# A graph network's edge layer without row gathers: all 50 node blocks in sorted buckets, part of the sort on GpSimd

## The reference

```python
x = layernorm(x + L0(x, src, dst))                    # mean of the sources, then a linear map
x = layernorm(x + L1(x, edge_weight, src, dst))       # two weighted propagations, L1A and L1B
x = layernorm(x + L2(x, edge_weight1, src, dst, ...)) # the edge layer
x = layernorm(x + L3(x, edge_index, ...))             # two SAGE layers, L3A and L3B

def L2(h, e, src, dst, W1, b1, W2, b2):
    m = relu(concatenate([h[src], h[dst], e]) @ W1 + b1) @ W2 + b2
    return segment_sum(m, dst)
```

## Time and profile before

| | us |
|---|---|
| three runs: lowest, median, highest | 3682.96, 3688.67, 3693.33 |
| profiled execution: span from the first to the last instruction | 4015.9 |
| its stages (us from the start): build and L0 | 260 to 1262 |
| L1A and L1B, first to last dense block, with the sort beside | 1262 to 2152 |
| edge layer, with what leads to and from it | 2152 to 3552 |
| L3A and L3B | 3552 to 4016 |
| busy of the span: PE, DVE, POOL, ACT | 3290.8, 2244.4, 1153.0, 1011.7 |

### The profile page before, as it was taken

One profiled execution on the slowest core, in us unless ns is written; L12 is line 12 of the kernel. 1 busy time (PEld: TensorE's weight loads), 2 busy tenths in 40 slices (PEclk: granted clock), 3 DMA queues, 4 the chain that ended last, 5 costly groups with the idle time before them and its releaser, 6 DMA issues.

```text
span 4015.9 us, 126981 instructions
## 1 busy us (share of the span) xinstructions
PE 3290.8 (82%) x56384; PEld 3021.5 (75%) x56384; DVE 2244.4 (56%) x3103; ACT 1011.7 (25%) x2184; POOL 1153.0 (29%) x1012
## 2 busy tenths in 40 slices
PE   0768999999997888888886577777787777789998
PEld 0757999999996888888885466665566565689898
DVE  8974777666767767677776234444454444331122
ACT  0025777777771000000000111111111111110000
POOL 5587000000001000001001665565566555501100
PEclk9987999999997999999997677777778777799999
DMA  4315777777776999988885343343344433369798
GB/s 122 98 38 179 280 282 278 269 275 269 282 284 242 381 394 381 382 362 345 344 357 192 83 108 107 102 113 104 100 117 109 114 100 104 99 275 343 297 372 326
DMA packets 285688, 904.33 MB, mean 225 GB/s; under 512 B 97944, under 2 KB 162702, under 8 KB 256850
## 3 DMA queue, kind: packets, MB, share of 16 engines
q1 hardware_dynamic: 235802, 857.37, 55.4%
q0 software_dynamic: 35520, 36.44, 6.7%
q10 hardware_dynamic: 13832, 2.70, 0.4%
HBM read 644.17 MB, written 252.83 MB: 223 GB/s over the span
## 4 chain that ended last, share of the span: by engine, by line
PE 39%; issue 35%; DVE 9%; DMA 6%; POOL 4%; another core or an unknown queue 2%; POOLq 2%; DVEq 2%; SPq 1%; ACT 0%; ACTq 0%
PE ps L1601 10%; PE ps L1418 7%; PE ps L1413 5%; DMA stream<-a_weights 5%; PE ps L1632 4%; PE ps L1596 4%; PE ps L1635 4%; PE ps L1521 2%; POOL wend L909 2%; POOL stream L916 2%; DVE operand_room L2274 1%; DVE junk L1739 1%; DVE operand_room L2291 1%; DVEq L2299 1%
## 5 line engine op out<-in xcount | busy, mean ns | idle before, releaser
L936 POOL DMA_INDIRECT stream<-table,stream x660 | 794.4, 1204 | 544.9 <-PE ps L1601 322.6
L1370 PE MATMUL ps<-operand_room 64*128 64x50 bf16 (+1 forms) x18750 | 645.6, 222 | 50.4 <-issue 18.1
L1370 PEld LDWEIGHTS ps<-operand_room 64*128 64x128 bf16 x18750 | 618.9, 163 | 81.8 <-issue 29.6
L1418 PE MATMUL ps<-stream,node_room 125*64 125x125 f32 x10000 | 579.2, 277 | 60.2 <-DMA stream<-a_weights 51.1
L1418 PEld LDWEIGHTS ps<-stream,node_room 125*64 125x64 f32 x10000 | 557.2, 140 | 70.9 <-DMA stream<-a_weights 57.5
L1074 ACT CAST stream<-ps 128x500 bf16<-128x500 f32 (+2 forms) x700 | 431.0, 632 | 246.1 <-PE ps L1370 193.2
L1074 ACT COPY stream<-ps 128x500 f32<-128x500 f32 (+2 forms) x700 | 421.5, 618 | 0.0
L1215 ACT ACTIVATE node_room<-ps 128x320 f32<-128x320 f32 x300 | 131.3, 438 | 885.7 <-remote 460.3
L1413 PE MATMUL ps<-operand_room,stream 125*125 125x192 bf16 x3750 | 319.2, 247 | 4.4 <-POOLq L578 4.4
L1413 PEld LDWEIGHTS ps<-operand_room,stream 125*125 125x125 bf16 x3750 | 313.5, 137 | 4.7 <-POOLq L578 4.7
L2356 DVE TENSOR_TENSOR node_room<-slot_f,stream 128x625 f32<-128x625 f32 x240 | 184.1, 809 | 210.9 <-remote 177.6
(11 more groups left out here) (292 smaller groups left out, 4518.3 us busy)
## 6 DMA issues: line engine op xcount, KB each, us to landing
stream<-a_weights SPq DMA_DIRECT2D x100, 3125.0 KB, 15.0
a_weights<-stream SPq DMA_DIRECT2D x500, 312.5 KB
stream<-a_counts SPq DMA_DIRECT2D x100, 1562.5 KB, 9.1
a_counts<-stream SPq DMA_DIRECT2D x500, 156.2 KB
stream<-sorted_edges SPq DMA_DIRECT2D x80, 781.2 KB
node_room<-sorted_edges SPq DMA_DIRECT2D x40, 781.2 KB
stream<-dst_run SPq DMA_DIRECT2D x20, 1031.2 KB
stream<-table,stream POOLq DMA_INDIRECT x660
```

The source lines that it names most:

```text
L936: pool.indirect_dma_start(emsg[s][:, t, :], None, tables[L2][:, :], bass.IndirectOffsetOnAxis(src_t[j % 3][:, at:at + 1], 0))\
L1370: ins = pe.matmul(out if step == 0 else out[:, 1:2], low[s][rows_a, :, t], planes[s][rows_a, t // TI, what, :, t % TI], start=step == 0, s ...
L1418: ins = pe.matmul(ps_sum[SUM_BANK[MATRIX[k]][b]][half:half + D, 0:Q], tab_in_of(k)[0:Q, h, :], a[0:Q, h, :], start=h < 2, stop=h >= NPP - 2)
```

## The change

All 50 blocks are done from sorted buckets. The gathers, the spread of the destination's half and the second relu go, with the run's loads and the stores of the node table and of the split edge values that served them. A *chunk* is now half a block: 5 units of 5 buckets, 100 chunks and 500 units in all; the one-hot rows of a chunk come in one broadcast of 12.8 KB rows to 125 partitions (cut at partition 112), compared against one key. The slot one-hots (of which destination a sorted edge has) are made by VectorE in bf16 for a whole chunk and cast to f32 by GpSimd (units 0, 2, 4 of a chunk) and ScalarE (1, 3), 625 elements each. The sums are in one bank a block, taken block by block.

The sort now does 50 blocks beside 100 dense blocks: `sort_with(n)` puts a half after each. The value splits (`sort_values`) and the product and the folds of the ranks (`fold`, the former L2278 to L2283) are GpSimd's; VectorE keeps the one-hots, the counts, the scan and the products with the values, and waits on `rank_rdy` before it makes the one-hot of the ranks. `hot_src`, `hot_pair` and `run_rank` are double, `run_val` and the keys three deep.

```diff
+        def fold(eng, b):
+            places, pair = hot_src[b % 2], hot_pair[b % 2]
+            ranks = places[:, :, 2:TPAD].rearrange("p s (u t) -> p s u t", t=2)
+            eng.tensor_tensor(ranks, ranks, pair.rearrange("p u s t -> p s u t"), ALU.mult)
+            eng.drain()
+            for to, n, of in ((0, 25, 25), (0, 12, 12), (0, 6, 6), (0, 3, 3), (0, 1, 1), (2, 1, 24)):
+                eng.tensor_tensor(places[:, to:to + n], places[:, to:to + n], places[:, of:of + n], ALU.add)
+                eng.drain()
+            eng.tensor_tensor(run_rank[b % 2].unsqueeze(1), places[:, 0:1, 2:TPAD], places[:, 2:3, 2:TPAD], ALU.add)
+            eng.drain()
...
-            def gather_runs():
...
+            def fold_ranks(b):
+                pool.wait_ge(ranks_counted, b + 1)
+                fold(pool, b)
+                pool.sem_inc(rank_rdy, 1)
+            def beside_weights():
+                for n in range(2 * NPP):
+                    if n % 2 == 0 and n // 2 + 2 < NPE:
+                        sort_values(n // 2 + 2)
+                    if n == 0:
+                        fold_ranks(0)
+                    if n % 2 and n // 2 + 1 < NPE:
+                        fold_ranks(n // 2 + 1)
+                    g = (n - NPP) // GT
+                    if n % GT == GT - 1 and n >= NPP + GT:
                         split_dst(g - 1)
+                split_dst(GROUPS - 1)
...
+            def sort_after(n):                       # TensorE, after dense block n
+                s = n // 2
+                if n % 2:
+                    sort_half(s, 0)
+                    if s:
+                        pe.wait_ge(base_used, min(s + 2, NPE))
+                        sort_slots(s - 1)
+                else:
+                    if n:
+                        sort_half(s - 1, 1)
+                    if s + 1 < NPE:
+                        sort_base(s + 1)
...
+                for w in range(UNITS + 1):           # TensorE, the edge layer
+                    if w < UNITS:
+                        unit(w)
+                    if w:
+                        collect_unit(w - 1)
...
+            def sort_vals(b, h):                     # VectorE
                 if h == 0:
+                    v.wait_ge(rank_rdy, b + 1)
...
+            def sort_with(n):                        # VectorE
+                s = n // 2
+                if n % 2:
+                    sort_vals(s, 0)
+                    if s + 1 < NPE:
+                        sort_counts(s + 1)
+                else:
+                    if n:
+                        sort_vals(s - 1, 1)
+                    else:
+                        sort_counts(0)
+                    if s + 1 < NPE:
+                        sort_pairs(s + 1)
```

More of the change, by code:

```diff
@@ L241, in build_program @@
[L241 to L247, removed]
@@ L255, in build_program @@
[L255 to L257 removed]
+        at = 2 * AROW // 2
+        hots = [in_room(stream, room(HW // 2), HW, BF16) for _ in range(HRING - 1)]
+        hots.append(in_room(node_room, 2 * NPP * D, HW, BF16))
+        slot_key = [in_room(node_room, PWORDS + GT * D + i * NPP, 2 * NPP, BF16).rearrange("p (s t) -> p s t", t=2)
+                    for i in range(3)]
@@ L595, in pieces_out, with turn_of, acc_copies, loads_of @@
             return moves
-        def turn_of(k, mode):
-            return ps_t
+        def turn_of(k, mode, j):
+            if k == L1B and mode == "linear" and j == GT - 1:
+                return bank(3)[:, GT * D:GT * D + P]
+            return ps_t[:, j * P:(j + 1) * P]
+        def acc_copies(b):
+            return sum(a % GT != GT - 1 for a in range(b + 1))
+        def loads_of(c):
+            return 16 * sum(3 + (a % 2 == 0) for a in range(c % HRING, c + 1, HRING))
         def both(eng, run):
@@ L1600, in add @@
-                def add(sums, m, half, rows_of, hots, first, last):
-                    return pe.matmul(sums[half * D:(half + 1) * D, m * Q:(m + 1) * Q], rows_of, hots,
-                                     start=first, stop=last)
-                def collect(c):
-                    i = c // CPB
-                    pe.wait_ge(slot_rdy, c + 1)
-                    pe.wait_ge(relu_done, c + 1)
-                    if c % CPG == 0 and c:
-                        pe.wait_ge(turned_sb, count(WITH_CAT, L2, c // CPG - 1))
-                    for t in range(CHUNK):
-                        at = c % CPB * CHUNK + t
-                        ins = add(ps_acc[0], i % POG, at % 2, emsg[c % MSGS][:, t, :], hot_slot[c % SLOTS][:, t, :],
-                                  at < 2, at >= TILES - 2)
-                    ins.then_inc(s_done, 1)
@@ new lines, in weights_pass @@
+            def weights_pass(k):
+                first = (L1A, L1B).index(k) * NPP
+                for g in range(GROUPS):
+                    for b in range(GT):
+                        if b == 1 and g:
+                            take_sums(k, g - 1, "linear")
+                            finish(k, g - 1, "linear")
+                        sort_with(first + g * GT + b)
+                        if b == GT - 1 and g and k == L1B:
+                            dst_half(g - 1, "linear")
+                        if k == L1A and g == 0 and b == GT - 1:
+                            edge_weights()
+                take_sums(k, GROUPS - 1, "linear")
+                finish(k, GROUPS - 1, "linear")
+                if k == L1B:
+                    sort_with(2 * NPP)
```

880 lines of the change are left out of this document (344 added, 536 removed).

## The result

The changed kernel takes 4001.97 us (median of 4 runs, 3995.78 to 4003.64) against 3687.76 for the kernel before in the same set: 1.0853 times as long, interval 1.0835 to 1.0872. The prediction was 3809, range 3570 to 3910: right in sign, two fifths of the size (+121 for +314), and the time lies above the range. The changed kernel's own profiled execution has a span of 3998.9 us, in line with its runs.

What follows compares the result with a forecast made beforehand. Weights stage taken as near the limits of TensorE and the `a_weights` stream, edge layer as TensorE and GpSimd's gathers holding each other up. 4016 - 470 (edge layer) + 270 (weights stage) + 5 (rest) - 12 (span over runs) = 3809 us; range 3570 to 3910.

Steps and rivals of the forecast that it cites:

- Span and runs: Kernel before: span 327.2 us above the runs, put down to 314.9 us of TensorE gaps in the profiled execution only.
- Rival B: Edge layer: TensorE's gaps are real in every run, so -470 counts against 3689, giving 3494 us; chance 0.08.
- The edge layer, 906: Edge layer: 500 units of 1.78 us at full clock plus 14 us, TensorE setting the pace; 906 for 1376, -470 us.
- The outer bound of +300 for half clock: Edge layer: a third of the units at half clock would cost some 300 us.
- Rival C: Weights stage: TensorE waits for the rank one-hot each pair of blocks, drops to 1.2 GHz; +150, 3959 us; chance 0.12.
- TensorE's added sorts, +55 to +109: Weights stage: 20 more sorts take TensorE 109 us; alone they make the stage some 55 to 109 us longer.
- "half" of cover: Weights stage: at best half of the added sorts' 109 us fits into TensorE's 108 us of idle time.
- rival A: Weights stage: folds hidden in VectorE's gaps, TensorE with the stream sets the stage at 956; 3605 us; chance 0.25.
- The exclusion, +270: Weights stage: two-input instructions of GpSimd and VectorE exclude each other, their sum 23.0 us a block; stage 1160, +270 us.
- The price of 8.0 us a block: Weights stage: GpSimd's product and folds, some 3460 elements in 8 instructions, priced 7.8 to 9.3 us, taken as 8.0.
- The wait that it names: Weights stage: the chain counts, fold, rank one-hot, with VectorE waiting for GpSimd, comes to 22.6 us and confirms the sum.
- The rest, +5: Outside both stages: the histogram's larger one-hot in the preparation adds 5 us; tables, edge-value split and dropped DMAs about nothing.

Runs made afterwards that it cites:

- Experiment 10: Changed kernel with product and folds still on GpSimd, but the rank one-hot takes stale ranks and VectorE asks for their end two blocks later: 3999.72 us.
- The copies: Experiment 10 with GpSimd's product and folds replaced by one-input copies of the same elements: 3838.94 us.

## Why the prediction was off, by its steps

**Span and runs.** This step failed in its reading. "I take it that they belong to the profiled execution" rested on two numbers that agree by chance, 314.9 and 327.2. The gaps are in the plain runs of two sets too (4017 and 4013 against spans of 4015.9), and in a set at 3688 they are neither in the runs nor in the trace. Rival B ("gaps real in every run") was nearer in mechanism, for such sets, but its sum took all of the -470 off 3689, of which 1376 - 1060 = 316 were never in the 3689. The forecast's own sum went through the changed kernel's span and so didn't depend on this, but for the 12 us taken off its end: span and runs differ by 2 or 3 there, not 12. What the misreading cost was the comparison: from a before at 3688 the edge layer had 1060 - 906 = 154 to win, not 470, and the agreement of 316 with the gaps' 314.9 is chance as well. Of the 316, 204 are TensorE's busy time (1003.5 for 799.9, at a granted clock of 0.75 for 0.87) and 112 are idle time (372.5 for 260.1): the gaps go, but waits for VectorE of some 250 us take most of their place. TensorE's own work in the layer rises with the change, from 800 us to 906 at the full clock, so of its idle time only 260 - 106 = 154 us could be won.

**The edge layer, 906.** This is the step that took the time out of the range. It took 1052: the term mis-sized by +146, of the 193 between 3809 and 4002. The unit of 1.78 us was right: with fewer bytes the layer takes 911. What failed is "A chunk's broadcast ... 4.5 us. So TensorE sets the pace, and as it doesn't idle I take the full clock". The loads are hidden as a wait and still cost 140 us, as gaps of TensorE with no releaser, multiples of 256 of its instructions apart, and the half clock behind them. The outer bound of +300 for half clock covered it; the value taken didn't. Rival C had it only as a remark.

**TensorE's added sorts, +55 to +109.** The stage without folds is +28, below the bound; it also lacks the folds of 30 blocks that VectorE has in the stage before. TensorE did get 82 us more work (862 for 780), but 54 of them went into idle time. The prediction's "half" of cover was too little. Of rival A only TensorE's part stands, and is below its 956 (913 measured); the folds are not hidden.

**The exclusion, +270.** It was +328, and without the folds +28: 300 us are the folds on GpSimd, shown by taking them out. The price of 8.0 us a block was right: the shortest of each of the eight instructions in the changed kernel's trace are 3.49, 1.75, 1.00, 0.59, 0.36, 0.24, 0.24 and 0.25 us, 7.9 in all (single instructions, from the order of time). VectorE's own share too: 754.5 us busy without folds is 15.1 us a block, and 15.1 + 7.9 = 23.0. The block took 1213 / 50 = 24.3 for a forecast of 23.2. The step that failed is "The cast at 1780.13, one input, took its usual 0.45 beside the same product". The earlier trace rows show that it began 0.03 us before VectorE's product: it was first, and so wasn't held. Nor is it a matter of two inputs on VectorE's side: the instruction that rows 9 show held for 0.57 us, L2240, has one input. From the misreading came "two-input instructions of the two engines exclude each other", and of the ten small instructions of a block's value splits only those with two inputs were in the sum. In the changed kernel they queue behind VectorE's long instructions (3.37 and 2.31 us for the two groups above; 0.21 and 0.31 us at the least), which delays the next fold, whose product then stands before the next one-hot. That this makes up the last 1.1 us a block is argued, not shown: no run took the splits out with the folds left on GpSimd, and the idle gaps of 0.14 us between the folds' instructions, which the prediction had as "partly on it", come to 1.0 us a block too (50 us over the 50 folds in the same stretch).

The Trainium skill has a fuller rule on another page than the one that the prediction read: "SBUF — State Buffer", section Who interferes with whom, says that a VectorE instruction with two SBUF inputs contends with a GpSimd instruction that reads SBUF, with no condition on how many inputs that one has, and that the order of issue, not the shape of the operation, decides which of the two blocks. The copies (+112 us) and the 34-element cast of 3.61 us agree with it.

**The wait that it names.** The prediction let the chain counts, fold, rank one-hot confirm its sum, and the profile after shows 172 us of VectorE waiting for the fold. Experiment 10 takes that wait away, and the stage is 20 us shorter of 300. VectorE's waits for GpSimd fall from 213 us (172 for the folds, 41 for the splits) to 123, and its own instructions become 60 us longer (busy for 1006 for 946). The wait was for the most part a symptom; the sharing is the cost. How much of the changed kernel's wait would stay if the two engines didn't hold each other up, no run shows.

**The rest, +5.** +7 up to the first dense block, in the set where both were traced. Right for the sum; its parts weren't tried.

In sum: 3809, +146 for the edge layer, +53 for the weights stage (323 for 270, both against the earlier trace rows), +12 and 2 at the end, and about -20 because that trace of before lies in a set where all kernels start the weights stage some 20 us later: 4002.

## What to carry to other kernels

Work moved from VectorE to GpSimd runs beside VectorE's only as far as VectorE's own instructions there aren't held. Here its two-input products were, and a scaling with one input too, while a copy of 320 f32 elements was not; one-input instructions of GpSimd held them just as two-input ones did. So read it from a trace, from the start times of both engines and not only the lengths. Where they do hold each other, take the sum of both: a block's sum of undisturbed lengths, 23.0 us, came within 1.3 us of the block. The same step cost twice on GpSimd what it cost on VectorE (300 for 146 us). When a span and the runs differ by hundreds of us, look for a second level of the kernel before calling it profiling, and check which terms of the forecast contain the difference. A load that is hidden by its ring can still slow TensorE; here half the bytes would have been worth 140 us of the stage.

## What the runs showed of the hardware that was not expected

The gathering kernel has two levels 9% apart, stable within a set of runs (13 runs within 0.9%, 13 within 1.2%, 19 within 1.5%). The changed kernel's medians of its two sets, both at the lower level, differ by 0.1%, and its two stages are as long in traces of the sets at the upper level. At the upper level TensorE shows 314.9 us of gaps beside indirect DMAs and a clock of 0.75; without the gathers they vanish. Whether it is the chip or where the tables lie in its memory is open: no run varied the place of a tensor.

TensorE's "issue" gaps with plain broadcasts (95 us at a DMA share of 0.60, one of 2.3 us at 0.33) are of another kind than those beside the gathers. Their distances are multiples of 256 records of TensorE's list without an exception, while of 551 distances between the gaps beside the gathers, over 0.2 us each, 460 are of 12 records or fewer. That TensorE's instructions come in blocks of 256 and that some blocks come late behind the broadcasts' data fits all of this, but no edit tried it by itself. The weights stage shows no such gaps, though it has a higher DMA share (0.88 with the folds left out); why it is spared is open.
